# A graph network kernel: own terms of sweep 1 made in its first strips, its combination without transposes, and single blocks added into the pairs' sums

## What is computed

```
T0 = h;  T1 = A h;  T2 = 2 A T1 - T0;  T3 = 2 A T2 - T1
x1 = x + T0 w0 + T1 w1 + T2 w2 + T3 w3          # Chebyshev layer
g  = relu(layernorm(x1));  deg = max(rowsum(A) + 1, 1)
z  = relu([g, (A g + g) / deg] @ W + b)         # SAGE layer
out = x1 + z / max(norm(z), 1e-12)
```

## Time and profile before

| | |
|---|---|
| median of 3 runs | 2425.84 us (2424.43 to 2427.28) |
| profiled execution | 2429.75 us, its span 2427.9 us |
| PE busy | 2100.9 us (87%) |
| DVE busy | 1660.0 us (68%) |
| POOL busy | 1347.6 us (56%) |
| ACT busy | 688.5 us (28%) |
| read from HBM | 698.55 MB, 289 GB/s over the span |

### The profile page before, as it was taken

The page is one execution under the profiler, slowest core; times in us unless marked ns, Lnnn a source line. Parts: engine busy times, 40 slices in busy tenths (PEclk is TensorE's granted clock), DMA queues, the critical chain, the costliest instruction groups (busy, mean ns, idle before and its releaser), DMA issues.

```text
span 2427.9 us, 29911 instructions
## 1 busy us (share of the span) xinstructions
PE 2100.9 (87%) x12104; PEld 1645.1 (68%) x12104; DVE 1660.0 (68%) x1260; ACT 688.5 (28%) x1667; POOL 1347.6 (56%) x1437
## 2 busy tenths in 40 slices
PE   2788889999999989999999867687888999977776
PEld 1455567788888867878888655566777777845554
DVE  7776887577776547665766454764666768588787
ACT  2444332443433146212123443511112221200010
POOL 5666665556555256357655262525574756667761
PEclk9898999999999999999999988888999999988898
DMA  9999999989988769689988787658896999999995
GB/s 280 365 359 347 352 350 361 327 294 347 326 295 305 240 170 297 235 290 299 321 268 308 218 227 235 203 179 291 262 278 219 362 323 339 305 363 318 300 261 155
DMA packets 225099, 702.67 MB, mean 289 GB/s; under 512 B 48834, under 2 KB 79554, under 8 KB 224962
## 3 DMA queue, kind: packets, MB, share of 16 engines
q0 software_dynamic: 168192, 664.89, 81.4%
q1 hardware_dynamic: 51776, 34.64, 5.7%
q10 hardware_dynamic: 4994, 1.25, 0.4%
HBM read 698.55 MB, written 2.10 MB: 289 GB/s over the span
## 4 chain that ended last, share of the span: by engine, by line
PE 72%; DVE 16%; DMA 4%; issue 3%; ACT 3%; POOL 2%; SPq 0%; DVEq 0%; ACTq 0%
PE ps_pair L736 51%; PE ps_single L742 14%; DVE ring L621 11%; DMA ring<-in_adj_dram,index 3%; ACT ring L441 2%; POOL ring L392 2%; PE ps_lin L700 1%; PE ps_lin L699 1%; PE ps_lin L684 1%; PE ps_lin L690 1%; PE ps_lin L695 1%; PE ps_lin L687 1%; PE ps_tr L703 1%; ACT sum_p L462 0%; DVE vec L491 0%
## 5 line engine op out<-in xcount | busy, mean ns | idle before, releaser
L392 POOL DMA_INDIRECT ring<-in_adj_dram,index x1424 | 1346.0, 945 | 1026.9 <-issue 402.9
L621 DVE STREAM_TRANSPOSE ring<-ring 128x2048 f32<-128x2048 f32 (+7 forms) x742 | 1478.9, 2053 | 164.0 <-ACT ring L441 142.0
L736 PE MATMUL ps_pair<-ring,vec 128*128 128x256 f32 x5760 | 1315.9, 389 | 108.2 <-DVE ring L621 83.2
L736 PEld LDWEIGHTS ps_pair<-ring,vec 128*128 128x128 f32 x5760 | 1109.5, 195 | 302.4 <-issue 111.1
L742 PE MATMUL ps_single<-ring,vec 128*64 128x256 f32 x4864 | 611.2, 405 | 183.5 <-DVE ring L621 177.8
L441 ACT ACTIVATE ring<-ring 128x1024 f32<-128x1024 f32 (+7 forms) x736 | 576.7, 787 | 432.9 <-DMA ring<-in_adj_dram,index 432.4
L742 PEld LDWEIGHTS ps_single<-ring,vec 128*64 128x64 f32 x4864 | 358.5, 145 | 405.8 <-issue 194.0
L460 ACT ACTIVATE sum_s<-ps_single 128x512 f32<-128x512 f32 x76 | 45.2, 594 | 932.4 <-PE ps_pair L736 469.4
L552 DVE TENSOR_TENSOR row_sums<-row_sums,more_sums 128x16 f32<-128x16 f32 x30 | 5.3, 178 | 312.5 <-PE ps_lin L696 166.3
L441 ACT ACTIVATION_READ_ACCUMULATOR ring<-ring 128x1 f32 x736 | 139.4, 189 | 0.0
L556 DVE TENSOR_TENSOR res<-res,ps_lin 128x256 f32<-128x256 f32 x16 | 6.7, 418 | 126.4 <-PE ps_tr L703 116.8
(11 more groups left out here) (79 smaller groups left out, 519.3 us busy)
## 6 DMA issues: line engine op xcount, KB each, us to landing
ring<-in_adj_dram,index POOLq DMA_INDIRECT x1424, 7.1
ring<-in_adj_dram SPq DMA_DIRECT2D x160, 96.0 KB, 2.7
ring<-in_adj_dram SPq DMA_DIRECT2D x160, 64.0 KB, 3.7
ring<-in_adj_dram SPq DMA_DIRECT2D x160, 32.0 KB
out_dram<-vec SPq DMA_DIRECT2D x64, 32.0 KB
res<-in_x_dram SPq DMA_DIRECT2D x4, 256.0 KB, 7.6
res<-in_x_dram ACTq DMA_DIRECT2D x4, 256.0 KB, 8.5
tmp<-in_L_gnn_weight_dram ACTq DMA_DIRECT2D x2, 64.0 KB
```

What stands on the lines that cost most here:

```text
L392: pool.indirect_dma_start(strip_of(i)[:, g, :], None, adj_q, bass.IndirectOffsetOnAxis(ap=index[:, 0:1], axis=0), element_offset=(QN * (g ...
L621: nc.vector.transpose(blocks, blocks).then_inc(s_turned, 1)
L736: last = nc.tensor.matmul(ps_pair[n % 2][:, cells], vec[:, CB * J + c, :, :], moving, start=(pair == 0), stop=(pair == pairs - 1))
```

## The change

1. The own term of sweep 1, T0 (w0 - w2), is no longer part of a row's combination. For all 16 rows it is made in the first 16 strips: PE makes `own_term(i)` and the transposes of the next vector ahead of the last unit of strip i, ACT copies, and DVE adds the term into `res` behind the second step of strip i + 1, for which it waits.
2. The combination of sweep 1 is eight instructions of 192 moving columns on `sum_p` (weights beside identities: the combination, the next vector and the partial sums come out side by side) and eight of 128 columns on `sum_s`. In sweep 2 those on `sum_p` have 128 columns. The transposes of `sum_p` go, and with them one DVE operation a row.
3. In rows with at most two single blocks a half, whose first and last block are pairs, single blocks accumulate straight into `ps_pair`, into the half of the partitions where the pairs' sums of the same product are. Such rows have no `ps_single` sums, no copy of them and no product with `sum_s`. They are row C = 14 of sweep 1, C = 13 to 0 of sweep 2, and C = 4, 6, 8, 12, 13 of sweep 3.
4. The PSUM tensors are laid out anew (`ps_out` over two banks, `ps_own`), and three weight tensors are cleared by POOL at the start where one was.

```diff
@@ -68,6 +68,7 @@
 BLOCK_COST = (0.86, 1.72)
 STORE_LAG = 12
 SINGLE, PAIR = 0, 1
+JOINED = 2
 LN_EPS = 1e-5
 L2_EPS = 1e-12
...
@@ -87,7 +88,11 @@
         self.units = sorted(early + behind, key=lambda unit: unit[0])
         kinds = {self.kind(J) for _, Js in self.units for J in Js}
         self.has_pair = PAIR in kinds
-        self.has_single = SINGLE in kinds
+
+        alone = [J for _, J0, w in pieces for J in range(J0, J0 + w) if self.kind(J) == SINGLE]
+        self.joined = self.has_pair and 0 < len(alone) <= JOINED * H and \
+            self.kind(self.units[0][1][0]) == PAIR == self.kind(self.units[-1][1][-1])
+        self.has_single = SINGLE in kinds and not self.joined
 
     def kind(self, J):
         if self.sweep == 4:
...
@@ -283,10 +289,21 @@
 
         ps_single = [ctx.enter_context(nc.psum_tensor(f"ps_single{i}", [P, BN], FP32)) for i in range(2)]
         ps_pair = [ctx.enter_context(nc.psum_tensor(f"ps_pair{i}", [P, BN], FP32)) for i in range(2)]
-        ps_lin = ctx.enter_context(nc.psum_tensor("ps_lin", [P, CB, 2, F], FP32))
-        ps_tr = ctx.enter_context(nc.psum_tensor("ps_tr", [P, CB, 2, F], FP32))
+        ps_out = ctx.enter_context(nc.psum_tensor("ps_out", [P, 2, BN], FP32))
         ps_xt = ctx.enter_context(nc.psum_tensor("ps_xt", [P, BN], FP32))
-        ps_deg = ctx.enter_context(nc.psum_tensor("ps_deg", [P, CH], FP32))
+        ps_own = ctx.enter_context(nc.psum_tensor("ps_own", [P, CB, F], FP32))
+        ps_deg = ps_own[:, 0, :]
+
+        def combined(c, first, last):
+
+            at = F * 3 * (c % 2)
+            return ps_out[:, c // 2, at + F * first:at + F * last]
+
+        def combination(k):
+            return ps_out[:, :, 0:2 * 3 * F].rearrange("p b (c k f) -> p b c k f", c=2, k=3)[:, :, :, k, :]
+
+        def by_bank(ap):
+            return ap.rearrange("p (b c) f -> p b c f", b=2)
 
         def strip_of(i):
...
@@ -423,6 +443,16 @@
             roots = 4
 
             summed = [0]
+            owns = [0]
+
+            def copy_own(strip):
+
+                while owns[0] < min(strip, NB):
+                    act.wait_ge(s_xt, owns[0] + 1)
+                    if owns[0]:
+                        act.wait_ge(s_own, owns[0])
+                    nc.scalar.activation(vec_t[0:F, :], ps_xt[0:F, :], ACT.Copy).then_inc(s_xtc, 1)
+                    owns[0] += 1
 
             def sum_rows(strip):
...
@@ -434,6 +464,7 @@
                     if row.sweep > 1 and extra_rows.index(n) >= 2:
                         act.wait_ge(s_degsum, extra_rows.index(n) - 1)
                     into = row_sums[:, row.C, :] if row.sweep == 1 else more_sums[:, extra_rows.index(n) % 2, :]
+                    copy_own(i)
                     for p in range(steps_of[i]):
                         act.wait_ge(*loads_of(i, p))
                         for g in range(GH)[groups_of(i, p)]:
@@ -448,10 +479,13 @@
                 if n + 1 < len(rows) and free_at[ahead] + 2 < row_start[n + 1]:
                     ahead += 1
                 sum_rows(ahead)
+                copy_own(first_strip[n + 1])
                 if n in x_rows:
-                    act.wait_ge(s_xt, x_rows.index(n) + 1)
+                    act.wait_ge(s_xt, NB + x_rows.index(n) + 1)
                     if x_rows.index(n):
                         act.wait_ge(s_lin, x_rows[x_rows.index(n) - 1] + 1)
+                    else:
+                        act.wait_ge(s_own, NB)
                     nc.scalar.activation(vec_t[0:F, :], ps_xt[0:F, :], ACT.Copy).then_inc(s_xtc, 1)
                 act.wait_ge(s_unit, row_start[n + 1])
                 if n:
...
@@ -555,19 +593,14 @@
 
                     nc.vector.tensor_tensor(x1, x1, lin, ALU.add)
                     if row.has_pair:
-                        nc.vector.tensor_copy(pt, tr[:, :, 1, :])
-                        then(nc.vector.tensor_copy(vec[:, sl, 1, :], new))
-                        last = nc.vector.tensor_tensor(vec[:, sl, 1, :], vec[:, sl, 1, :], tr[:, :, 0, :], ALU.add)
+                        nc.vector.tensor_copy(pt, partial)
                     else:
-                        nc.vector.memset(pt, 0.0)
-                        last = nc.vector.tensor_copy(vec[:, sl, 1, :], new)
+                        nc.vector.memset(part[:, sl, :], 0.0)
+                    last = nc.vector.tensor_copy(by_bank(vec[:, sl, 1, :]), new)
                 elif row.sweep == 2:
 
-                    then(nc.vector.tensor_tensor(x1, x1, lin, ALU.add))
-                    if row.has_single:
-                        then(nc.vector.tensor_tensor(tmp[:], pt, new, ALU.add))
-                    if row.has_pair:
-                        then(nc.vector.tensor_tensor(tmp[:], tmp[:] if row.has_single else pt, tr[:, :, 1, :], ALU.add))
+                    then(nc.vector.tensor_tensor(scratch, pt, new, ALU.add))
+                    nc.vector.tensor_tensor(x1, x1, lin, ALU.add)
                     last = nc.vector.scalar_tensor_tensor(out=vec[:, sl, 0, :], in0=tmp[:], scalar=2.0,
                                                           in1=vec[:, sl, 0, :], op0=ALU.mult, op1=ALU.subtract)
                 elif row.sweep == 3:
...
@@ -619,6 +652,11 @@
                         dve.wait_ge(s_summed, sums_to[sum_strips.index(i)] + p + 1)
                     blocks = strip_of(i)[:, groups_of(i, p), :].rearrange("p g (c q) -> p g c q", q=32)
                     nc.vector.transpose(blocks, blocks).then_inc(s_turned, 1)
+                    if 1 <= i <= NB and p == 1:
+                        own = res[:, CB * (i - 1):CB * i, :]
+                        dve.wait_ge(s_own, i)
+                        nc.vector.tensor_tensor(own, own, ps_own[:], ALU.add).then_inc(s_added, 1)
+                        dve.wait_ge(s_added, i)
                     step = steps_to[i] + p + 1
                     if ended < begun and step > end_step[ended]:
                         epilogue_end(ended)
...
@@ -646,18 +684,25 @@
                     pe.wait_ge(s_row, k)
                     stored[0] = k
 
-            def transpose_vector(n):
-
-                row = rows[n]
-                if row.sweep == 4:
-                    need_rows(row_index[3, row.C] + 1)
+            def transpose_vector(C, slot):
+
+                if slot == 1:
+                    need_rows(row_index[3, C] + 1)
                 if xts[0]:
                     pe.wait_ge(s_xtc, xts[0])
-                src_slot = 0 if row.sweep == 1 else 1
                 for c in range(CB):
-                    last = nc.tensor.transpose(ps_xt[0:F, P * c:P * c + P], vec[:, CB * row.C + c, src_slot, :], ident[:])
+                    last = nc.tensor.transpose(ps_xt[0:F, P * c:P * c + P], vec[:, CB * C + c, slot, :], ident[:])
                 last.then_inc(s_xt, 1)
                 xts[0] += 1
+
+            def own_term(C):
+
+                pe.wait_ge(s_xtc, C + 1)
+                if C:
+                    pe.wait_ge(s_added, C)
+                for c in range(CB):
+                    last = nc.tensor.matmul(ps_own[:, c, :], vec_t[0:F, P * c:P * c + P], rhs_x1[:], start=True, stop=True)
+                last.then_inc(s_own, 1)
 
             def epilogue(n):
...
@@ -679,28 +724,26 @@
                 for c in range(CB):
                     cols = slice(P * c, P * c + P)
                     S, PR, XT = sum_s[:, cols], sum_p[:, cols], vec_t[:, cols]
-                    lin, both = ps_lin[:, c, 0, :], ps_lin[:, c, :, :]
+                    lin, both, whole = combined(c, 0, 1), combined(c, 0, 2), combined(c, 0, 3)
                     if row.sweep == 1:
-                        nc.tensor.matmul(both, S, rhs_s1[:], start=True, stop=False)
                         if row.has_pair:
-                            nc.tensor.matmul(lin, PR, rhs_p1[:], start=False, stop=False)
-                        last = nc.tensor.matmul(lin, XT[0:F, :], rhs_x1[:], start=False, stop=True)
+                            last = nc.tensor.matmul(whole, PR, rhs_p1[:], start=True, stop=not row.has_single)
+                        if row.has_single:
+                            last = nc.tensor.matmul(both, S, rhs_s1[:], start=not row.has_pair, stop=True)
                     elif row.sweep == 2:
+                        if row.has_pair:
+                            last = nc.tensor.matmul(both, PR, rhs_p2[:], start=True, stop=not row.has_single)
                         if row.has_single:
-                            last = nc.tensor.matmul(both, S, rhs_s2[:], start=True, stop=not row.has_pair)
-                        if row.has_pair:
-                            last = nc.tensor.matmul(lin, PR, rhs_p2[:], start=not row.has_single, stop=True)
+                            last = nc.tensor.matmul(both, S, rhs_s2[:], start=not row.has_pair, stop=True)
                     elif row.sweep == 3:
                         if row.has_pair:
-                            nc.tensor.matmul(both, PR, rhs_p3[:], start=True, stop=False)
```

(22 more changed lines are left out.)

39 lines of the change are left out of this document (23 added, 16 removed).

## The result

The changed kernel takes 2438.6 us (median of 10 runs, 2429.68 to 2439.36), the kernel before 2426.17 (10 runs, 2423.52 to 2428.82): ratio 1.0043 with a 95% interval of 1.0035 to 1.0052. The forecast was 2430.7, 0.2% above the median known then; the ratio says 0.43%, and the two medians lie 12.4 us (0.5%) apart. The profiled executions lie closer together, 2437.02 against 2429.75, with spans of 2435.2 and 2427.9, 7.3 us apart.

What follows compares the result with a forecast made beforehand. Bounds: transfers and a PE-DVE loop in early rows, PE from 453 us, then a chain in sweep 2. 35.7 - 7 - 19.8 + 1.9 - 2.4 - 5 + 1.5 = +4.9 us, median 2430.7; range 2404 to 2444.

Steps and rivals of the forecast that it cites:

- Part 1: Own terms in the first 16 strips of sweep 1: +35.7 us, from +18.7 lateness and +17 PE clock.
- the loop: First 16 strips: DVE's addition waits for PE, PE for the transposes behind it; 11.8 us per strip against 8.8.
- Rows 4 to 8: Sweep 1, transfers at share 0.99: the shorter combination gives -7 us, bounds -2 and -16.
- Rows 9 to 15: Sweep 1, PE the bound: seven shorter combinations give -19.8 us, row 14's join costs +1.9.
- Sweep 2: -2.4 us at sweep 1's last row, then -5 together from joins (+19.6), smaller combinations (-18.8), dropped copies (-4), chain (-1.8).
- the surcharge: 0.21 us more in the unit behind a single block for the width switch; may go or stay.
- Sweeps 3 and 4: Five joined rows in sweep 3 cost +1.5 us, behind idle PE at best; no step in sweep 4.
- The clock stays up: Rival: PE's clock holds in the first rows, the same sum without the 17: 2413 us, chance 0.2.
- The waits hide: Rival: PE reaches own terms early enough or rows 4 to 8 recover wholly: about -30, 2396 us, chance 0.1.
- The join does not cost: Rival: eight instructions pipeline in one half at the old pace: about -29, 2401 us, chance 0.04.
- Slower: Rival: the loop of the first 16 strips costs more than PE's gains, part 1 over 40 us: 2443 us, chance 0.26.

Runs made afterwards that it cites:

- addition last: Changed kernel with DVE's addition of the own term behind the fourth transpose of the next strip, not the second: 2395.45 us, 0.9867 of before.
- the two-halves kernel: Changed kernel with joined blocks' products sent to both column halves in turn, output wrong: 2682.12 us, 0.9852 of before, among slow transfers.

## Why the prediction was right, and where its terms were off

**Part 1, the loop.** Forecast +35.7 us at row C = 3's end, measured +35.0. The loop's parts stand in the timelines: 11.49 us per strip at full clock (11.8 forecast), the eight products 1.03 (1.4), the four transposes 0.56 (0.5), DVE's wait 2.1 to 5.8 (2 to 4). The clock took what was forecast: from the second strip up to the row's end the first units of nine of the 15 strips that PE waits for are longer than at the full clock (in the lines above 7.09 and 7.47 instead of 5.40, and 5.36 instead of 3.67; a pair unit at 240.94 is the ninth), by 1.7 to 2.8 each, 17.4 us in all, against 10 of 12 strips by 1.7, 17 us. How the 35.0 divide between clock and order is read from rows and not separated by a run: when the order was mended, most of both went (clock 0.95 instead of 0.89). One reading of the prediction was loose, without harm to the sum: DVE does not stand until 193.11 us in the earlier trace rows; between the lines shown it turns 14 blocks in a row from 96.49 and 13 from 142.66.

**Rows 4 to 8.** Forecast -7, with bounds of -2 and -16: measured -7.4. Row C = 4 gave nothing (52.48 us against 52.31), the rows 5 to 8 gave 7.6, and in these transfers fill the time:

```profile
319.86:510.46 190.60, 174.59 (x1089) 132.77 (x1090) 145.34 (x76) 73.04 (x137) 119.91 (x128) 0.97 1.01 360
```

With the addition last, row C = 4 gave 3.6 and the five rows 11.4 us.

**Rows 9 to 15.** Forecast -17.9, measured -16.2. The combination's 2.19 us is the 2.2 of the sum. What was mis-sized here is the combination before. The 4.59 us come from the one combination whose four transposes of `sum_p` hold PE for 0.90 us; PE's clock is low there. In the other six rows they hold it for 0.49 or 0.50, as in the one below, and the combination is 4.19. The transposes of another row, then the clock at those of the earlier trace rows, both before:

```profile
652.30 0.66 PE L703 MATMUL ps_tr<-ident,sum_p 128*128 128x128 f32 x4
652.80 0.38 PE L736 MATMUL ps_pair<-ring,vec 128*128 128x256 f32 x1
```
```profile
705.90:706.90 1.00, 1.00 (x7) 0.93 (x7) 0.00 (x0) 0.00 (x0) 0.70 (x2) 0.57 0.99 344
```

So a row gave 4.19 + 0.44 - 2.19 = 2.44 us, and the rows 9 to 12 measure just that (2.44, 2.44, 2.44, 2.43). The missing 1.7 us are then: 2.4 in six rows of 0.4 each, 0.6 in the row C = 14, where the join cost 3.44 - 0.90 = 2.5 instead of 1.9, less 1.3 that the row C = 13 gave beyond its 2.8, since before it lost time to the clock and after it didn't.

**Sweep 2.** Forecast -2.4 - 5 = -7.4, measured -3.7 (514.7 against 518.5 us). This is the term with the largest miss, and the step is the price of a half block: eight instructions in one half were taken as eight pair instructions, 1.73 us, and whether the surcharge in the unit behind goes was left open, +0.7 in all. They take 1.87 and the surcharge stays, +0.86. Over 28 half blocks that is 4.5 us, the gap of 3.7 and a little more. By the forecast's own terms the join in sweep 2 was 19.6, less 14 x 0.9 for the dropped product, less 4 for the copy: +3. With 0.86 it is 24.1 - 12.5 - 3.8 = +7.8, and that is what the steady prices give for 14 rows (7.6).

The Trainium skill, "TensorEngine Tiling (Array Packing)", "Tiling Modes", says that a change of mode drains the engine and that different tiles work in parallel. The trace agrees with the second, 1.01 against 1.87 us for two halves or one, and is in line with the first: the unit behind takes 1.94 us instead of 1.73, joined or not.

What the forecast didn't see is the start of sweep 2. Without the join its first four rows (C = 15 to 12) are together 7.9 us shorter than before, where the shorter combination and DVE's part were given 1.8 + 2.4 for the whole change-over, and the rows C = 7 and 6 are 5.7 shorter (36.15 and 36.97 us against 38.63 and 40.17), where 0.9 was due for the two by the transposes gone (0.45 a row). The changed kernel keeps only a part of both. Its granted clock is 0.84 in C = 14 and 0.96 in C = 6, that of before 0.67 and 0.92, that of the kernel without the join 1.00 in both. It is tempting to put this down to the join, and the table above says no: without the join two kernels have 0.96 in C = 6 and one has 0.84 in C = 14, and with it two have 1.00 in both. So a part of the 13.7 us that the removal of the join gave in sweep 2, against 9.9 in the other pair, goes with the clock in these rows and not with the join. What lets the clock fall in the one kernel and not in the other is not known.

**Sweeps 3 and 4.** Forecast +1.5, measured -0.4 (lateness 7.7 at 1388 us, 7.3 at the end). That the join's cost there lies behind idle PE is likely and not shown.

**The total.** The terms give +4.9, the profiles +7.3: the five gaps of -0.7, -0.4, +1.7, +3.7 and -1.9 partly cancel. The other 5.5 us between forecast and median are in the profiled executions: that of before lies 3.9 us above the median that the forecast started from, that of after 1.6 below its own. Of the changed kernel's ten runs two are at 2430 and eight at 2437 to 2439, so a single execution could have said either; what makes the two groups isn't known.

**The rivals.** *The clock stays up* fell with the granted clock of 0.76 and units of 7.09 us. *The waits hide* fell with the additions' 47.6 us of idle. *The join does not cost* fell with 1.87 us, and the two-halves kernel shows the condition under which it would have held. *Slower*, priced at 2443, lies nearer to the median (4.4 us) than the forecast does (7.9), but by the wrong sum: part 1 stayed under its 40 us, and a part of the difference came from sweep 2.

## What to carry to other kernels

A small operation that waits for another engine is priced by what stands behind it in its queue: here 0.42 us of addition, placed two transposes too early, closed a loop between DVE and PE and cost 43 us; moved behind them, all work of the own terms in these strips together costs some 4 us. Price each part of a change against the kernel with all the other parts, not against the kernel before: the new combination saves PE nothing in a full row while the own term stays in it, and 2.44 us when it is out. The price of one part can also hold some luck of its neighbours: the join cost 5 us on the kernel before, 17 in the changed one and 12 with the addition last, and a part of the difference goes with PE's clock in two rows. Read an instruction's price from several rows, not from one: one row at the low clock gave 0.90 for 0.49. Sums that go to one column half in a row lose the overlap of the two halves, so folding a narrow block into a wide accumulation only pays if what it saves at the row's end is worth more than 0.86 us per eight instructions.

## What the runs showed of the hardware

- Eight instructions of 64 stationary columns took 1.01 us alternating between the halves and 1.87 in one half, which is more than eight of 128 columns (1.73).
- The loss by the clock is not a function of the idle before it alone: after 2.62 us of idle, 48 instructions took 7.09 us at 73.61 and 5.40 at 86.78, with the same work between.
- In row C = 14 of sweep 2 the granted clock was 0.84 in two kernels (10.78 us) and 1.00 in five others (9.14 us) whose row has the same 40 instructions on PE.
- A pair of instructions over 64 rows costs 0.36 us inside a combination, and lengthens the next product by 0.10 (0.33 to 0.43 from start to start); eight of them in a row took 1.03 in all.
- Transfers were slower for all kernels of one group of runs (before: 2722 us; the same kernel moved 261 GB/s there and 295 later). The cause is open.
